# Tokens transposed by DMA instead of TensorE and ScalarE, f32 second layers in three more slots, and a shifted order of ScalarE's side work

## What is computed

```
x = x + conv(layernorm_over_channels(x))      # super tokens: 8x8 cells, a 3x3 affinity softmax,
                                              # attention over 49 cells, spread back to the pixels
t = tokens(x);  s = layernorm(t)
probs = softmax(s @ gate_w + gate_b);  keep the top 2 of 4 experts, renormalised
h = gelu(einsum("bsd,edh->ebsh", s, w1) + b1)  # 96 -> 384
y = einsum("ebsh,ehd->ebsd", h, w2) + b2       # 384 -> 96
x = t + sum_over_experts(masked_probs * y)
```

## Time and profile before

| | |
|---|---|
| median of 3 runs | 548.12 us (547.88 to 549.78) |
| the profiled execution, its own time | 547.52 us |
| its span in the trace | 545.7 us |
| TensorE matmul busy | 515.4 us, 94% |
| VectorE busy | 420.0 us, 77% |
| ScalarE busy | 364.9 us, 67% |
| GpSimd busy | 110.9 us, 20% |
| DMA, mean | 32 GB/s |

### The profile page before, as it was taken

One profiled execution on the slowest core, in us unless ns is written; L12 is line 12 of the kernel. 1 busy time (PEld: TensorE's weight loads), 2 busy tenths in 40 slices (PEclk: granted clock), 3 DMA queues, 4 the chain that ended last, 5 costly groups with the idle time before them and its releaser, 6 DMA issues.

```text
span 545.7 us, 14434 instructions
## 1 busy us (share of the span) xinstructions
PE 515.4 (94%) x6006; PEld 382.5 (70%) x6006; DVE 420.0 (77%) x1087; ACT 364.9 (67%) x364; POOL 110.9 (20%) x189
## 2 busy tenths in 40 slices
PE   9798998899899999899899999899899999999995
PEld 5796865776577877676577787676576677766765
DVE  7474969788888587878888587867788877888775
ACT  1044169376867568676977468767878877888872
POOL 2230020123412320122511420120213400103000
PEclk9659579799999999999999999999999999999999
DMA  8942012000000004000000000000000000000000
GB/s 232 271 105 81 2 32 59 16 2 16 17 1 16 17 2 106 16 2 16 2 17 16 16 3 17 1 16 17 2 16 16 17 16 3 17 16 16 17 16 18
DMA packets 15719, 17.52 MB, mean 32 GB/s; under 512 B 13781, under 2 KB 13917, under 8 KB 15262
## 3 DMA queue, kind: packets, MB, share of 16 engines
q1 hardware_dynamic: 14626, 14.86, 10.0%
q10 hardware_dynamic: 1028, 1.74, 1.2%
HBM read 11.78 MB, written 4.82 MB: 30 GB/s over the span
## 4 chain that ended last, share of the span: by engine, by line
PE 74%; DVE 10%; ACT 7%; issue 5%; DMA 3%; SPq 0%; DVEq 0%; ACTq 0%
PE ps L1299 28%; PE ps L1328 14%; PE ps L1333 7%; PE ps L1151 5%; ACT h L669 4%; PE ps L1315 3%; DMA xt<-xtok 3%; PE ps L1320 3%; PE ps L1164 3%; PE ps L1131 2%; DVE xt L1008 2%; PE ps L1241 2%; PE ps L1253 1%; DVE affr L232 1%; DVE hl L992 1%
## 5 line engine op out<-in xcount | busy, mean ns | idle before, releaser
L669 ACT ACTIVATE h<-ps 128x1536 f32<-128x1536 f32 (+1 forms) x100 | 142.4, 1424 | 67.2 <-PE ps L1299 66.8
L992 DVE TENSOR_TENSOR hl<-h,hh 128x1536 f16<-128x1536 f32 x94 | 168.1, 1788 | 22.0 <-issue 16.4
L1299 PE MATMUL ps<-xhl,w_hi 97*128 97x512 f16 (+1 forms) x672 | 177.9, 355 | 0.0
L677 ACT CAST hh<-h 128x1536 f16<-128x1536 f32 x94 | 137.7, 1465 | 3.0
L1008 DVE SCALAR_TENSOR_TENSOR xt<-ps,gl,xt 128x96 f32<-128x96 f32 (+1 forms) x400 | 99.9, 309 | 50.8 <-PE ps L1333 45.3
L1299 PE MATMUL ps<-xhl,w_lo 97*128 97x512 f16 (+1 forms) x336 | 114.4, 354 | 0.0
L1328 PE MATMUL ps<-w_lo,hh 128*128 128x96 f16 x1128 | 108.1, 207 | 0.0
L1328 PE MATMUL ps<-w_hi,hh 128*128 128x96 f16 x1128 | 108.1, 207 | 0.0
L1328 PEld LDWEIGHTS ps<-w_lo,hh 128*128 128x128 f16 x1128 | 97.7, 98 | 6.3 <-issue 0.2
L1328 PEld LDWEIGHTS ps<-w_hi,hh 128*128 128x128 f16 x1128 | 99.0, 98 | 3.3
L1299 PEld LDWEIGHTS ps<-xhl,w_hi 97*128 97x128 f16 x672 | 57.2, 100 | 48.2 <-issue 2.1
(11 more groups left out here) (164 smaller groups left out, 500.3 us busy)
## 6 DMA issues: line engine op xcount, KB each, us to landing
xch<-x SPq DMA_DIRECT2D x4, 1176.0 KB, 7.5
out<-xt SPq DMA_DIRECT2D x24, 192.0 KB, 2.1
xt<-xtok SPq DMA_DIRECT2D x4, 663.0 KB, 13.5
xt<-xtok SPq DMA_DIRECT2D x4, 612.0 KB, 11.2
h<-w ACTq DMA_DIRECT2D x2, 576.0 KB
wqkv_sb<-wqkv ACTq DMA_DIRECT2D x1, 228.0 KB
tab<-table ACTq DMA_DIRECT2D x1, 117.0 KB, 4.8
out<-xt SPq DMA_DIRECT2D x4, 24.0 KB, 1.8
```

Of the source, the lines that this page charges most:

```text
L669: act.activation(h32[:, i % 3, :, 0:width(i)], z, ACT.Gelu, scale=1.0 / WS).then_inc(S["h_ready"], 1)
L677: act.copy(hh[:, i % 3, :, 0:width(i)], h32[:, i % 3, :, 0:width(i)]).then_inc(S["hh_ready"], 1)
L992: dve.tensor_tensor(hl[:, i % 2, :, 0:n], h32[:, i % 3, :, 0:n], hh[:, i % 3, :, 0:n], ALU.subtract).then_inc(S["hl_ready"], 1)
L1299: ins = pe.matmul(ps[:, CH * (i % 2) + c, k * m:(k + 1) * m], ww[:, w0:w0 + 128], xhl[:, b % 2, half, r * UT:r * UT + m], start=(n == 0), ...
```

## The change

- **Transposes.** SyncE issues one DMA transpose for each unit (28 in all), from `x16` (now padded to 128 columns a tile) to `xhl` (now 128 partitions, by tile, half and token). The row of ones that carries the first layer's bias comes from a column of `x16` that GpSimd sets once, and no longer from a load. TRN pieces and `tokens_turned` are gone. Each transpose waits until the one before has landed.
- **f32 second layers.** `whole(i)` holds for slots 0, 1 and 2 of image 0 too.
- **Order.** TABLE and SHORT move some pieces; ScalarE reads a half-0 piece of the next slot directly after the slot's `hidden_high`, ahead of its small work; `affinity_quotient` comes in slot 1 instead of 2; GpSimd's `affinity_weights` waits for `affr_ready`; for image 3 the first two units are normalised one slot sooner (`unit_slot`).
- **End.** The second-last slot's second layer uses the side bank (`sum_bank`).

```diff
 def whole(i):
-    return (i % SLOTS == SLOTS - 1 and i < ALL - SLOTS) or (i % SLOTS == 0 and i > 0)
+    return i < 3 or (i % SLOTS == SLOTS - 1 and i < ALL - SLOTS) or (i % SLOTS == 0)
...
-        x16 = sb("x16", [PT, T, 2, C], F16)
-        xhl = sb("xhl", [CB, 2, 2, IMG], F16)
+        x16 = sb("x16", [PT, T, 2, 128], F16)
+        xhl = sb("xhl", [128, 2, T, 2, PT], F16)
...
-        EARLY = {(1, 1): (0, "TRN", 1), (3, 0): (0, "TRN", 2),
-                 (3, 1): (1, "SFT", 0, 0, 4), (4, 0): (1, "SFT", 0, 1, 4), (4, 1): (1, "SFT", 0, 2, 4),
+        EARLY = {(3, 1): (1, "SFT", 0, 0, 4), (4, 0): (1, "SFT", 0, 1, 4), (4, 1): (1, "SFT", 0, 2, 4),
...
-                 (9, 1): (1, "PRO", 0), (10, 0): (1, "PRO", 1), (10, 1): (1, "AFT", 0), (11, 0): (1, "AFT", 1),
-                 (11, 1): (1, "PIX", 0), (12, 0): (0, "TRN", 4), (12, 1): (1, "PIX", 1), (20, 1): (0, "TRN", 6),
-                 (22, 1): (1, "TRN", 0)}
+                 (9, 1): (1, "PRO", 0), (10, 0): (1, "PRO", 1), (10, 1): (1, "AFT", 0), (11, 1): (1, "PIX", 0),
+                 (12, 0): (1, "AFT", 1), (12, 1): (1, "PIX", 1), (13, 1): (1, "PIX", 2)}
...
+        def unit_slot(b):
+            return 20 if b + 2 < B else 19
...
+        def sum_bank(i):
+            return SIDE if i == ALL - 2 else Y
...
+            def turn_tokens(b, u):
+                sp.wait_ge(S["xhi_ready"], b * G + u + 1)
+                sp.wait_ge(S["xlo_ready"], b * G + u + 1)
+                if u == 0 and b >= 2:
+                    sp.wait_ge(S["z_done"], (b - 1) * SLOTS)
+                sp.wait_ge(S["turned"], (b * UNITS + u) * 16)
+                t0, t1 = tiles(u)[0], tiles(u)[-1] + 1
+                sp.dma_start(xhl[:, b % 2, t0:t1, :, :], x16[:, t0:t1, :, :], transpose=True).then_inc(S["turned"], 16)
...
+            sp.wait_ge(S["pool_set"], 8)
+            turn_tokens(0, 0)
+            turn_tokens(0, 1)
             for b in range(B):
                 if b + 2 < B:
                     sp.wait_ge(S["side_done"], number[last_logits(b + 1)] + 1)
                     load_channels(b + 2)
...
+                for slot in range(SLOTS):
+                    if slot - 1 in NORMAL:
+                        turn_tokens(b, NORMAL[slot - 1])
+                    if slot % E == 0 and slot > 0:
+                        store(b, slot // E - 1)
+                    if b + 1 < B and slot - 1 in (unit_slot(b), unit_slot(b) + 1):
+                        turn_tokens(b + 1, slot - 1 - unit_slot(b))
...
             def affinity_weights(b):
-                pool.wait_ge(S["scale_ready"], 2 * b + 2)
+                pool.wait_ge(S["affr_ready"], 2 * b + 2)
...
-                for half in range(2):
-                    if read_at(b, slot, half):
-                        side_read(read_at(b, slot, half))
+                if read_at(b, slot, 1):
+                    side_read(read_at(b, slot, 1))
                 if i + 2 < ALL:
                     hidden_full(i + 2)
                     hidden_high(i + 2)
+                after = divmod(i + 1, SLOTS) + (0,)
+                if i + 1 < ALL and read_at(*after):
+                    side_read(read_at(*after))
                 if slot in NORMAL:
                     tokens_high(b, NORMAL[slot])
...
                 if b + 1 < B:
-                    if i == 2:
+                    if i == 1:
                         affinity_quotient()
...
                 if e == 0:
-                    pe.wait_ge(S["side_act"], reads_up_to((b, "TRN", r)))
+                    pe.wait_ge(S["turned"], (b * UNITS + r + 1) * 16)
...
-                if i > 0:
-                    pe.wait_ge(S["sum_done"], i)
+                if sum_bank(i) == SIDE:
+                    pe.wait_ge(S[reader_of(visits[-1][0])], reads_up_to(visits[-1][0]))
+                elif i > 0:
+                    pe.wait_ge(S["sum_done"], i if sum_bank(i - 1) == Y else i - 1)
```

More of the change, by code:

```diff
@@ L259, in build @@
         READER = {"SF": "act", "CEN": "act", "LOG": "dve", "SFT": "dve", "AFT": "act", "SUPT": "act", "QKV": "dve",
-                  "SCO": "dve", "PRT": "act", "HEA": "dve", "HET": "act", "PRO": "dve", "PIX": "dve", "TRN": "act"}
+                  "SCO": "dve", "PRT": "act", "HEA": "dve", "HET": "act", "PRO": "dve", "PIX": "dve"}
         ROTATE = (SIDE, Y, 5, 4, 3)
@@ L428, in _ @@
                     load_channels(b + 2)
-                for u in range(UNITS):
-                    first, n = b * IMG + u * UT, unit_tokens(u)
-                    sp.wait_ge(S["sum_done"], b * SLOTS + min(SLOTS, (u + 1) * E))
-                    sp.dma_start(out[first:first + n, :].rearrange("(t p) c -> p t c", p=min(n, PT)),
-                                 rows_of(b, u)[:, :, 0:C]).then_inc(S["out_stored"], 16)
+                for slot in range(SLOTS):
[5 more added lines that the diff above has]
+                        turn_tokens(b + 1, slot - 1 - unit_slot(b))
+                store(b, UNITS - 1)
             sp.wait_ge(S["out_stored"], B * UNITS * 16)
@@ L621, in tokens_high @@
                     act.wait_ge(S["xlo_ready"], (b - 1) * G + r + 1)
-                    act.wait_ge(S["side_done"], number[(b - 1, "TRN", r)] + 1)
+                    act.wait_ge(S["turned"], ((b - 1) * UNITS + r + 1) * 16)
                 rows = slice(tiles(r)[0], tiles(r)[-1] + 1)
-                act.copy(x16[:, rows, 0, :], xs[:, rows, :]).then_inc(S["xhi_ready"], 1)
-            def tokens_turned(b, r):
-                bank = opened((b, "TRN", r))
-                if r == 0 and b >= 2:
-                    act.wait_ge(S["z_done"], (b - 1) * SLOTS)
-                n = unit_tokens(r)
-                act.copy(xhl[0:C, b % 2, :, r * UT:r * UT + n],
-                         bank[0:C, 0:n].bitcast(F16).rearrange("p (h n) -> p h n", h=2)).then_inc(S["side_act"], 1)
+                act.copy(x16[:, rows, 0, 0:C], xs[:, rows, :]).then_inc(S["xhi_ready"], 1)
             def gate_exponentials(b):
@@ L655, in side_read @@
                     projected(b, k)
-                elif kind == "TRN":
-                    tokens_turned(b, k)
             def hidden_full(i):
@@ L1243, in pixels @@
                 ins.then_inc(S["side_done"], 1)
-            def turn_tokens(b, r):
-                pe.wait_ge(S["xhi_ready"], b * G + r + 1)
-                pe.wait_ge(S["xlo_ready"], b * G + r + 1)
-                o = bank((b, "TRN", r))
-                for half in range(2):
-                    for j, t in enumerate(tiles(r)):
-                        n = tokens_of(t)
-                        c0 = (half * unit_tokens(r) + j * PT) // 2
-                        ins = pe.transpose(o[0:C, c0:c0 + n // 2].bitcast(F16), x16[0:n, t, half, :], ident16[0:n, 0:n])
-                ins.then_inc(S["side_done"], 1)
             def side(v, part=0, parts=1):
@@ L1283, in side @@
                     pixels(b, k)
-                elif kind == "TRN":
-                    turn_tokens(b, k)
             def first_layer(i):
@@ L1294, in first_layer @@
                 m = unit_tokens(r)
+                t0, t1 = tiles(r)[0], tiles(r)[-1] + 1
                 for c in range(CH):
@@ L1395, in lay @@
         return np.ascontiguousarray(np.asarray(a))
-    table, inner, cells, near, ones = constants()
+    table, inner, cells, near = constants()
     wqkv = np.asarray(L0_conv_qkv_w).reshape(HEADS, 3, HD, C).transpose(3, 1, 0, 2)
@@ L1413 @@
         "near": near,
-        "ones": ones,
         "wqkv": lay(wqkv),
```

58 lines of the change are left out of this document (29 added, 29 removed).

## The result

| | before | after |
|---|---|---|
| median, 4 runs each | 548.95 us (547.88 to 550.24) | 529.73 us (528.09 to 531.40) |
| ratio, 95% interval | | 0.9649 (0.9609 to 0.9689) |
| the profiled execution, its own time and span | 547.52, 545.7 | 530.16, 528.4 |

The kernel is 19.2 us faster by the medians, 17.3 by the two profiled spans. The forecast of 529 was right as a whole, and part of that is luck: in the trace, 2.5 us more than forecast were gained in two stretches and 3.9 less in two others.

What follows compares the result with a forecast made beforehand. TensorE, busy 94% of the span, was taken as the bound. Terms 8.9 + 2.9 + 4.9 + 2.6 + (5.2 - 1.9) - 4.0 = 18.6 off 547.5 gave 529 us, with 80% from 521 to 541.

Steps and rivals of the forecast that it cites:

- X, the transpose: Time of one 256 KB DMA transpose, SBUF to SBUF, taken as 5 us; slow transposes (7 to 10) had chance 0.12.
- The term of 1.9 for the start: Bare DMA transpose ahead of the first layer at the kernel's start: first layer at 73.9, 1.9 us later than before.
- The margin at the image starts: Time from low part to first layer of an image's first unit, about 6 us; only a longer transfer costs there.
- Transposes off TensorE with ScalarE's copies: Token transposes leaving TensorE save 8.9 us; ScalarE's copies going, with GpSimd's weights behind the scaling, save 2.9.
- The 3 x 0.45 taken off for slot 7: Transposes in slot 7 of three images, ahead of a wait for VectorE's softmax: no gain counted, 3 x 0.45 us.
- The wait for the scaled affinities (1.43): TensorE's wait ahead of the super tokens in two images: goes, 2 x 1.43 = 2.9 us.
- Order of the side work: Images 0 to 2: slot 11's pixels' wait of 1.12 gone, about 0.5 of AFT's 1.08 gone; 4.9 us in three images.
- The term of 4.9: Forecast gain in us over three images from reordering the side work around the second AFT, the pixels and PRO's read.
- VectorE takes back: VectorE has the same 100 us of work in 5 us less per image: 1 to 1.5 us lost an image, 4 in all.
- The end: Last two slots: waits of 1.15 and 1.09 for bank Y go; VectorE's last sum starts some 2.6 us sooner.
- First stage: Image 0, slots 0 to 2: super tokens at 95.5 for 98.11 and no low clock, 2.6 + 2.6 = 5.2 us.
- Runs of 128 columns: First layer's reads in runs of 128 columns in place of 512: nothing; 4 us lost if they cost 2%.

Runs made afterwards that it cites:

- e1: The changed kernel with image 3's first two units normalised in slots 20 and 21, as in the other images; 527.45 us, ratio to before 0.9601.
- e6: By elimination (label not tied explicitly): the changed kernel with the second-last slot's second layer in bank Y again; 529.79 us, ratio to before 0.9638.
- e7: The changed kernel with the second AFT piece back in slot 11's first half, ahead of the pixels; 527.49 us, ratio to before 0.9587.
- e8: The changed kernel with image 3's first units normalised from slot 20 and pieces PRT to first AFT half a slot later; 520.95 us, ratio to before 0.9476.

## Why the prediction was right, point by point

The time came out by a sum in which misses went both ways: the order of the side work was taken some 2 to 3 us too high, the transfer 1.6 too dear and what VectorE takes back too high in the images, and a loss at the start of image 3 was not seen. The mechanisms held, but for the order and for that unseen place.

- **X, the transpose: right in kind, too large.** 5 was taken, 3.1 measured from issue to landing and 3.45 from low part to first layer, nearer still to the store's 2.1. The term of 1.9 for the start is 0.3. The margin at the image starts was given as 6; in after the first unit's low part ends at 187.63 and its first layer starts at 195.25, 7.6, since GpSimd's low part takes 0.91 there and not 2.44. Two transposes fit in, but for 0.26 once; three do not. What the prediction did not see is that a transpose can stand behind a store on SyncE: at the start of image 3 the low part ends at 416.72, the store goes out at 417.77 and the transpose at 418.74, 2.0 late, which costs nothing in after. Of the two figures of the Trainium skill the one in "Advanced Engine Details and Errata", X-Bar Transpose, as fast as a plain transfer, is the nearer: 3.1 for 256 KB beside 2.2 for a store of 192 KB. The 1309 ns for each 128 x 128 in "VectorE: DVE Perf Modes", The three transpose paths, does not add up over a transfer of eight; the estimate from it was 10.5.
- **Transposes off TensorE with ScalarE's copies: right**, 8.2 by putting them back for 8.9, 9.9 without the stretch at the start of image 3. The 3 x 0.45 taken off for slot 7 is there too: PRT waits 0.80 and not 0.35. The wait for the scaled affinities (1.43) goes, but mostly by GpSimd's later start: it is 0.97 with that undone (1.1 of each step), 0.29 with the transposes and copies undone.
- **Order of the side work: the step that failed.** "The second AFT leaves the place ahead of slot 11's pixels, which is the wait of 1.12: gone." That wait went, and one of 0.53 came ahead of the second AFT, for VectorE's `xt`: the piece now stands behind pixels that VectorE reads. The move by itself is worth 0.2 and not 1.12, since without it the wait is 0.71; ScalarE's order gives 0.4 (forecast 0.5). The term of 4.9 is some 1.8 over three images by undoing its parts, and 3.0 by the waits for pixels and AFT, before less after.
- **VectorE takes back: an even 4.0 was the wrong shape.** In the images TensorE waits 0.53 for VectorE ahead of the second AFT, 1.6 in three, and the steps gained 1.3 more than forecast. Where it took most was one place that the prediction did not name, the start of image 3: 2.7 us by `e1`, 1.3 to 1.6 of it clock, through a `normalise` that comes a slot sooner and waits for GpSimd. "About the same" was said of these units' margin, with an eye on the transfer alone; the edit's inputs were not looked up.
- **The end: right**, 2.6 forecast, 2.3 measured.
- **First stage: right, and hidden in after's own trace.** The low clock behind the idle of 3.56 is gone, as forecast (2.6, near what the first of the two steps gained beyond the second: 8.1 less 5.4). The count gave 23.4 us from the first layer to the super tokens (72.07 to 95.5). `e6`, `e7` and `e8` have 23.4 to 23.6, after has 24.4 and before 26.0. From low part to super tokens that is 2.2 to 2.3 less than before's 29.17, the forecast's 2.6 less 0.3 for the transfer; in after it is 1.3, beside a lower clock in the first 100 us, below.
- **Runs of 128 columns: nothing**, as forecast: nine matmuls of a first layer take 1.94 as before.

The trace leaves one thing open. 2.3 us of a step are not the transposes; 1.1 (GpSimd), 0.4 (ScalarE's order) and 0.2 (AFT) are shown one by one, and 0.6 is not assigned. 0.4 of it can be seen as the pixels' wait that is 0.71 in `e7` and was 1.12, with a cause that no run isolates. The quotient one slot sooner, in image 0's slots, was not undone by itself either.

## What to carry to other kernels

A wait that is taken away between two engines uncovers the next one behind it, here at half its size: price an order change by following both engines through the next three pieces, and not by the wait that it removes. When a step is moved a slot earlier, look up each input's producer in the trace, the quiet engine's too: behind 1.13 us of GpSimd's lateness stood 2.4 of TensorE's wait and, in some executions, more at the low clock. Once the transposes were off TensorE, half a slot more of distance between dependent pieces, with slot 20 for image 3, gave another 1.7% (520.95 for 529.73; 1.8% by the ratios to before); try the order again after every structural change.
